# Sixteen routing weights per token: from selector products on TensorE to a DRAM row read back by DMA, with the preparing chain two steps earlier

## The chip, the cores and the metric

The kernel runs on one core of a Trainium2 chip as one program. The metric is the device time of one execution in microseconds; the times below are of separate executions of the same program.

## What is computed

The model has two layers on 2048 tokens of width 128: an attention layer with a mixture of eight experts, then a state-space mixer with a gated MLP, and at the end the mixture that this change touches. Cut to that last part (x is 2048 x 128, E = 16 experts, K = 8 of them chosen, plus one shared expert that every token uses):

```python
scores   = sigmoid(x @ gate_w.T)                 # 16 per token
inds     = top_k(scores + expert_bias, 8)
selected = scores[inds] / sum(scores[inds]) * 2.826
combine  = one_hot(inds) @ selected              # 16 weights per token, 8 of them zero
h        = silu(x @ w_gate[e].T) * (x @ w_up[e].T)
y        = sum_e combine[:, e] * (h[e] @ w_down[e].T)
y        = y + (silu(x @ shared_gate.T) * (x @ shared_up.T)) @ shared_down.T
out      = layernorm(x + y)
```

The kernel computes all sixteen experts for all tokens and multiplies the hidden activations of expert e by the token's weight for e before the down product.

## The kernel before

All of the change is in `mixer_tail_stage`, the last of the kernel's stages. It works on four blocks of 512 tokens (b = 0 to 3). The activations lie transposed, features on the 128 partitions and the 512 tokens of a block along the free dimension, so a token's routing weight has to be present on all partitions as a row of 512 numbers, one row per expert.

In each block there are 17 steps (x = 0 to 16, `NX`); step 0 is the shared expert and the others are experts 0 to 15. On TensorE a step has, in this order: the gate product (L1629, written G below), the up product (L1632, U), for x above 0 the selector product (L1639, S), and the down product of the step before (L1648, D). A number behind the letter is the step whose data it works on, so step 14 issues G14, U14, S14, D13. After step 16 an eighteenth turn of the loop (x = 17) has only D16. G, U and D are fp32 products of 128 x 128 weights with 512 columns, each two matmul instructions. S is one bf16 matmul: a 96 x 128 matrix of ones and zeros (`sel`) picks the row of one expert out of `cparts`, which holds the 16 x 512 weights in three bf16 parts on partitions 0, 32 and 64, and writes their sum on all 128 partitions of PSUM bank 4.

ScalarE applies silu to the gate product (L1755). VectorE multiplies it by the up product (L1906) and then by the spread weights in bank 4 (L1911, result `hid`); the two together are `hidden(b, x)`, and its end is called h of that step. S waits for h of the step before, since it overwrites bank 4, and so does D.

Between the steps of block b the chain that prepares block c = b + 1 is laid out by hand, with one piece per step on each engine in its own order. Its pieces before the change, with the step x behind which each stands on its engine:

- `turn_xs` (TensorE, 0), `copy_xs` (ScalarE, 1), `mean_squares` (VectorE, 0), `project` (TensorE, 2), `residual` (VectorE, 2), `square2` (ScalarE, 4), `mean_squares2` (VectorE, 4), a power on GpSimd (L1510), `scale` (VectorE, 6, L1835)
- `turn_n` (TensorE, 7), `copy_n` (ScalarE, 7), `gate_up`, `silu3` and `gated` (TensorE, ScalarE, VectorE, 8 to 10), `project_down` and `add_mlp` (11), `mean` (VectorE, 12), `apply` (ScalarE, 13), `turn_x` and `copy_x` (14)
- `route` (TensorE, 15, L1599), `sigmoid` (ScalarE, 15), `choose` (VectorE, 15, the top 8 of 16 and the normalised weights), `turn_c` (TensorE, 17, L1607), `parts` (VectorE, 16, L1884 to L1892)

From block 1 on, `turn_back` (TensorE, 4, L1619), `finish` (VectorE, 4, L1916), a power on GpSimd, `mean_out` (VectorE, 6) and `apply_out` (ScalarE, 7) finish block b - 1, and the sync engine stores it (L1499). `turn_xs` waits until `parts` of the block has read bank 7. All waits between engines are semaphores; an engine executes its own list in order, so a waiting instruction holds everything behind it.

Of the kernel before, what the change touches and what calls it, by code (L numbers as in the profile page):

```python
# [16 lines left out]
P = 128  # L17
# [1424 lines left out]
def mixer_tail_stage(g, m, out, eps=1e-5, eps_rms=1e-6):  # L1442
# [7 lines left out]
    with ExitStack() as ctx:  # L1450
# [18 lines left out]
        total = g.sb(ctx, "t3_total", [P, 4])  # L1469
        rest = g.sb(ctx, "t3_rest", [RE, 512])  # L1470
        cparts = g.sb(ctx, "t3_cparts", [96, 2, 512], BF16)
        sel = g.sb(ctx, "t3_sel", [96, RE * P], BF16)
        hid = g.sb(ctx, "t3_hid", [P, 2, 512])
# [10 lines left out]
        x_ps, x_sb, logits, sig = S_("x_turned"), S_("x_copied"), S_("logits"), S_("sigmoid")  # L1484
        routed, choice, c_turned, c_step, c_done = (S_(x) for x in ("route_step", "choice", "c_turned", "c_step", "c_parts"))
        zeroed, sel_in = S_("zeroed"), S_("sel_in")
        gu_ps, c_ps, acted, used, h_done, down = (S_(x) for x in ("gate_up", "c_spread", "silu", "used", "hid", "down"))
        out_sb, back, fin, var2, rstd2, nb2, sent = (S_(x) for x in ("out_copied", "back", "fin", "fvar", "frstd", "fmean", "final"))
# [3 lines left out]
        with nc.Block() as block:  # L1492
            @block.sync
            def _(sp):
                sp.dma_start(g.XW[:], g.aps["experts"]).then_inc(g.experts_in, 16)
                sp.dma_start(g.sel[:], g.aps["select"]).then_inc(g.experts_in, 16)
                for b in range(NB):
                    sp.wait_ge(sent, 4 * b + 4)
                    sp.dma_start(out.rearrange("o (t p) e -> p (o t) e", p=P)[:, 4 * b:4 * b + 4, :],  # L1499
                                 blk(g.X, b)).then_inc(stored, 16)  # L1500
                sp.wait_ge(stored, 16 * NB)

            @block.gpsimd
            def _(pool):
                half4 = g.half[:, 0:4]
                pool.memset(cparts[:], 0.0).then_inc(zeroed, 1)

                def power(dst, src, due, b, done):
                    pool.wait_ge(due, b + 1)
                    pool.tensor_tensor(dst, src, half4, ALU.pow).then_inc(done, 1)  # L1510
# [24 lines left out]
            def _(pe):  # L1535
                def turn_xs(b):

                    if b:
                        pe.wait_ge(sig, b)
                        pe.wait_ge(c_done, 5 * b - 1)  # L1540
                        if b >= 3:
                            pe.wait_ge(fin, b - 2)
# [79 lines left out]
                def products(b, x):  # L1622

                    e, k = order[x], NX * b + x
                    if k == 0:
                        pe.wait_ge(g.experts_in, 32)
                    if k >= 2:
# [4 lines left out]
                    pe.matmul(ps[:, 2 + k % 2, :], xw("up", e), XT[:, b % 2, :], start=True, stop=True).then_inc(gu_ps, 1)  # L1632
                    if x:
                        if x == 1:
                            pe.wait_ge(c_done, 5 * b + 5)
                        if k == 1:
                            pe.wait_ge(sel_in, 1)
# [22 lines left out]
                for b in range(NB):  # L1660
                    c = b + 1
                    for x in range(NX + 1):
# [22 lines left out]
                        if x == 17:  # L1685
                            turn_c(c)
# [3 lines left out]
            def _(act):  # L1690
# [86 lines left out]
                for b in range(NB):  # L1777
                    c = b + 1
                    for x in range(NX):
# [11 lines left out]
                        if x == 4:  # L1791
                            square2(c)
                        if x == 7:
                            copy_n(c)
                        if 8 <= x <= 10:
                            silu3(c, x - 8)
                        if x == 13:
                            apply(c)
                        if x == 14:
                            copy_x(c)  # L1800
                        if x == 15:
                            sigmoid(c)
# [4 lines left out]
            def _(dve):  # L1807
                stats = Count(stepped)
                routing = Count(routed)
                c_count = Count(c_step)  # L1810

# [63 lines left out]

                def parts(b):

                    part = lambda n: cparts[32 * n:32 * n + RE, b % 2, :]
                    dve.wait_ge(c_turned, b + 1)
                    if b == 0:  # L1880
                        dve.wait_ge(zeroed, 1)
                    if b >= 2:
                        dve.wait_ge(c_ps, RE * (b - 1))
                    dve.tensor_copy(part(0), B[0:RE, :]).then_inc(c_done, 1)  # L1884
                    dve.wait_ge(c_done, 5 * b + 1)
                    dve.tensor_tensor(rest[:], B[0:RE, :], part(0), ALU.subtract).then_inc(c_done, 1)
                    dve.wait_ge(c_done, 5 * b + 2)
                    dve.tensor_copy(part(1), rest[:]).then_inc(c_done, 1)
                    dve.wait_ge(c_done, 5 * b + 3)
                    dve.tensor_tensor(rest[:], rest[:], part(1), ALU.subtract).then_inc(c_done, 1)  # L1890
                    dve.wait_ge(c_done, 5 * b + 4)
                    dve.tensor_copy(part(2), rest[:]).then_inc(c_done, 1)  # L1892

                def hidden(b, x):
# [37 lines left out]
                choose(0)  # L1932
                parts(0)
                for b in range(NB):
                    c = b + 1
                    for x in range(NX):
# [11 lines left out]
                        if x == 4:  # L1948
                            mean_squares2(c)
                        if x == 6:  # L1950
                            scale(c)
                        if 8 <= x <= 10:
                            gated(c, x - 8)
                        if x == 11:
                            add_mlp(c)
                        if x == 12:
                            mean(c)
                        if x == 15:
                            choose(c)
                        if x == 16:  # L1960
                            parts(c)
                finish(NB - 1)
# [7 lines left out]
def layers(nc, aps, out):  # L1970
    with ExitStack() as ctx:
# [32 lines left out]
        with ExitStack() as mctx:  # L2004
# [10 lines left out]
            with ExitStack() as xctx:  # L2015
                g.XW = g.sb(xctx, "experts_w", [P, X_N])
                g.sel = g.sb(xctx, "select", [96, RE * P])
                g.experts_in = g.sem("experts_in")
                mixer_tail_stage(g, m, out)


def host_layout(inputs):
# [44 lines left out]
    for name in ("ident", "mask_qk", "mask_kq"):  # L2067
# [18 lines left out]
        "rope_cos": c32(cos), "rope_sin": c32(sin),  # L2086
        "select": np.repeat(np.tile(np.eye(32, RE), (3, 1)), P, axis=1).astype(np.float32),
    }
# [14 lines left out]
```

## Time and profile before

| what | value |
|---|---|
| median of 3 runs | 1882.82 us (1882.42 to 1883.24) |
| the profiled execution, its own time | 1885.1 us |
| its span, first to last instruction | 1883.3 us |
| TensorE busy | 1666.7 us, 88% |
| VectorE busy | 1335.5 us, 71% |
| ScalarE busy | 1141.9 us, 61% |
| GpSimd busy | 200.9 us, 11% |
| mean granted TensorE clock | 0.929 |

The last stage begins at about 1596 us of the span. Its four blocks of expert steps run from 1634 us to 1874 us. The span is 1.8 us shorter than the execution's own time, and that time is 2.3 us above the median of the runs. Matmul records overlap: a record lasts longer than the slot that the instruction takes in the queue, so slots are read from start to start.

### The profile page before, as it was taken

The numbers are of one execution on the slowest core, as the hardware profiler recorded it, in microseconds if no ns is written. First come the engines' busy times: TensorE is split into PE (matmuls) and PEld (weight loads), VectorE is DVE, ScalarE is ACT, GpSimd is POOL, SyncE is SP. The second block draws the span as 40 slices with busy tenths as digits, with TensorE's granted clock in tenths as the row PEclk, the third lists the DMA queues.
The fourth block names the chain that finished last, engine by engine and source line by source line (L and its number), as shares of the span: only waits on it lengthen the run. The fifth ranks groups of instructions, "written<-read, shape, count | busy, mean of one in ns | idle before, by whom it ended". The sixth has DMA issues, their size and how long they took to land. (4 is left out here: it accounts for less than half of the span.)

```text
span 1883.3 us, 25598 instructions
## 1 busy us (share of the span) xinstructions
PE 1666.7 (88%) x9916; PEld 795.1 (42%) x9916; DVE 1335.5 (71%) x1849; ACT 1141.9 (61%) x2305; POOL 200.9 (11%) x160
## 2 busy tenths in 40 slices
PE   6699999999999998857999999999794376699998
PEld 4233333333333333343444444455562344344443
DVE  4988888888888886258788677674474676355654
ACT  5078888888888887741677877777444511333432
POOL 1000000000000100110010001111522041100100
PEclk9699999999999999967899999999897777799999
DMA  2000000000000000010000000000000000100000
GB/s 94 0 1 1 1 1 1 1 1 1 1 1 1 1 1 1 1 45 0 1 1 1 1 1 1 2 1 2 1 1 0 0 1 27 61 1 6 6 1 12
DMA packets 4665, 13.32 MB, mean 7 GB/s; under 512 B 344, under 2 KB 2400, under 8 KB 4192
## 3 DMA queue, kind: packets, MB, share of 16 engines
q1 hardware_dynamic: 4544, 11.68, 1.9%
q8 instruction: 79, 1.29, 0.3%
q14 instruction: 42, 0.34, 0.1%
HBM read 10.63 MB, written 1.05 MB: 6 GB/s over the span
## 5 line engine op out<-in xcount | busy, mean ns | idle before, releaser
L636 DVE TENSOR_REDUCE a_part_max<-a_ps 128x2 f32<-128x1024 f32 x512 | 602.1, 1221 | 85.2 <-PE a_ps L495 84.4
L621 ACT ACTIVATE a_probs<-a_ps 128x512 f32<-128x512 f32 x1024 | 532.7, 615 | 128.7 <-PE a_ps L553 126.4
L636 DVE TENSOR_REDUCE f_part_max<-f_ps 128x2 f32<-128x1024 f32 (+3 forms) x320 | 327.3, 1061 | 121.6 <-PE f_ps L495 65.3
L553 PE MATMUL a_ps<-a_q_shift,a_KA 64*128 64x512 f32 x1024 | 366.0, 446 | 3.9 <-POOL a_q_shift L476 2.7
L621 ACT ACTIVATE f_probs<-f_ps 128x512 f32<-128x512 f32 (+3 forms) x640 | 300.3, 538 | 99.1 <-PE f_ps L553 48.6
L495 PE MATMUL a_ps<-a_KA,a_q_open 64*128 64x512 f32 x1024 | 285.0, 484 | 14.5 <-DVE a_part_max L636 13.8
L553 PEld LDWEIGHTS a_ps<-a_q_shift,a_KA 64*128 64x128 f32 x1024 | 166.9, 186 | 289.0 <-ACT a_probs L621 274.0
L571 PE MATMUL a_psO<-a_probs,a_VA 128*32 128x512 f32 x2048 | 274.6, 608 | 3.9 <-ACT a_probs L621 3.9
L553 PE MATMUL f_ps<-f_q_shift,f_KA 64*128 64x512 f32 (+3 forms) x640 | 222.9, 434 | 4.8 <-ACT f_probs L621 2.2
L495 PE MATMUL f_ps<-f_KA,f_q_open 64*128 64x512 f32 (+3 forms) x640 | 175.2, 452 | 17.0 <-DVE f_part_max L636 16.2
L553 PEld LDWEIGHTS f_ps<-f_q_shift,f_KA 64*128 64x128 f32 x640 | 106.6, 188 | 148.9 <-ACT f_probs L621 138.9
L495 PEld LDWEIGHTS a_ps<-a_KA,a_q_open 64*128 64x128 f32 x1024 | 124.7, 191 | 96.9 <-DVE a_part_max L636 77.3
L571 PE MATMUL f_psO<-f_probs,f_VA 128*32 128x512 f32 (+3 forms) x1280 | 152.2, 548 | 0.1
L1755 ACT ACTIVATE t_prod<-t_ps 128x512 f32<-128x512 f32 x68 | 40.6, 597 | 129.1 <-PE t_ps L1629 129.1
L476 POOL TENSOR_TENSOR a_q_shift<-a_q_open,a_shift_row 128x512 fp32r<-128x512 f32 x32 | 40.2, 1278 | 661.0 <-ACT a_shift_row L614 661.0
L495 PEld LDWEIGHTS f_ps<-f_KA,f_q_open 64*128 64x128 f32 x640 | 83.7, 196 | 44.9 <-DVE f_part_max L636 31.9
L1906 DVE TENSOR_TENSOR t_prod<-t_prod,t_ps 128x512 f32<-128x512 f32 x64 | 43.9, 687 | 68.7 <-PE t_ps L1632 68.7
L476 POOL TENSOR_TENSOR f_q_shift<-f_q_open,f_shift_row 128x512 fp32r<-128x512 f32 x32 | 40.1, 1275 | 424.3 <-ACT f_shift_row L614 424.3
L1648 PE MATMUL t_ps<-t_hid,experts_w 128*128 128x512 f32 x136 | 69.9, 594 | 5.2 <-DVE t_hid L1911 5.2
L1629 PE MATMUL t_ps<-t_XT,experts_w 128*128 128x512 f32 x136 | 70.6, 601 | 0.0
L1632 PE MATMUL t_ps<-t_XT,experts_w 128*128 128x512 f32 x136 | 70.3, 599 | 0.0
L571 PEld LDWEIGHTS a_psO<-a_probs,a_VA 128*32 128x32 f32 x2048 | 40.5, 108 | 70.6 <-issue 31.4
(311 smaller groups left out, 1765.2 us busy)
## 6 DMA issues: line engine op xcount, KB each, us to landing
experts_w<-in_experts SPq DMA_DIRECT2D x1, 3264.0 KB, 12.6
W<-in_weights SPq DMA_DIRECT2D x1, 2086.0 KB, 10.5
out<-X SPq DMA_DIRECT2D x4, 256.0 KB, 2.3
select<-in_select SPq DMA_DIRECT2D x1, 768.0 KB, 13.9
K<-in_consts SPq DMA_DIRECT2D x1, 644.0 KB, 7.0
R<-in_rows SPq DMA_DIRECT2D x1, 530.0 KB, 6.1
X<-in_x SPq DMA_DIRECT2D x1, 0.5 KB, 6.4
C<-in_cols SPq DMA_DIRECT2D x1, 15.0 KB, 5.3
```

The costliest lines, as they stand in the source:

```text
L476: pool.tensor_tensor(q_shift[:, u % 2, jp, :], q_open[:, u % 2, jp, :].bitcast(F32), shift_row[:, u % 2, :], ALU.add).then_inc(q_shifted, 1)
L495: mm = pe.matmul(ps1[:, k % 2, x, 0:b - a], q_open[rows, u % 2, jp, P * q:P * q + P], g.KA[rows, 2 * n + jp, a:b], start=True, stop=not diag)
L553: mm = pe.matmul(bank(r)[:, lo:512], g.KA[rows, 2 * n + jp, P * s:P * s + P], q_shift[rows, u % 2, jp, lo:512], start=True, stop=not diag)
L571: mm = pe.matmul(psO[32 * j:32 * j + 32, lo:hi], g.VA[:, s, VW * h:VW * h + 32], probs[:, st % 2, j, lo:hi], start=(s == 0), stop=(s == pl ...
L621: nc.scalar.activation(probs[:, st % 2, j, lo:512], bank(r)[:, lo:512], ACT.Exp, scale=SCALE).then_inc(ring_read, 1)
L636: dve.tensor_reduce(part_max[:, 4 * q + 2 * jp:4 * q + 2 * jp + 2, c], ps1[:, k % 2, :, 0:b - a], AX_X, ALU.max).then_inc(max_read, 1)
L1629: pe.matmul(ps[:, k % 2, :], xw("gate", e), XT[:, b % 2, :], start=True, stop=True).then_inc(gu_ps, 1)
L1632: pe.matmul(ps[:, 2 + k % 2, :], xw("up", e), XT[:, b % 2, :], start=True, stop=True).then_inc(gu_ps, 1)
L1648: pe.matmul(ps[:, 5, :], xw("down", order[x]), hid[:, k % 2, :], start=(x == 0), stop=(x == NX - 1)).then_inc(down, 1)
L1755: nc.scalar.activation(prod[:, k % 2, :], ps[:, k % 2, :], ACT.Silu).then_inc(acted, 1)
L1906: dve.tensor_tensor(p, p, ps[:, 2 + k % 2, :], ALU.mult).then_inc(used, 1)
```

## The change

The selector products, their matrix, and the splitting in three bf16 parts are removed. `copy_c` on VectorE copies the 16 x 512 weights of a block from PSUM to SBUF. The sync engine stores them to a DRAM tensor `c_rows` (32 KB), waits for the store, and reads them back onto all 128 partitions in four DMAs of four experts each (1 MB per DMA, 8 KB per partition) into `c_all`, which holds two blocks. `hidden` takes its second factor from `c_all`, and waits for one of the four DMAs at x = 1, 5, 9 and 13. From `turn_n` on the chain stands two steps earlier, `scale` one step earlier. The stores of results on the sync engine stand behind the weights' DMAs of two blocks on.

```diff
@@ sync engine
                 sp.dma_start(g.XW[:], g.aps["experts"]).then_inc(g.experts_in, 16)
-                sp.dma_start(g.sel[:], g.aps["select"]).then_inc(g.experts_in, 16)
                 for b in range(NB):
+                    sp.wait_ge(c_sb, b + 1)
+                    sp.dma_start(g.c_rows[b], cT[:, b % 2, :]).then_inc(c_out, 16)
+                    sp.wait_ge(c_out, 16 * b + 16)
+                    if b >= 2:
+                        sp.wait_ge(h_done, NX * (b - 1))
+                    for e in range(0, RE, 4):
+                        sp.dma_start(c_all[:, b % 2, e:e + 4, :],
+                                     g.c_rows[b, e:e + 4].partition_broadcast(P)).then_inc(c_in[e // 4], 16)
+                    if b < 2:
+                        continue
+                    sp.wait_ge(sent, 4 * b - 4)
+                    sp.dma_start(out..[:, 4 * b - 8:4 * b - 4, :], blk(g.X, b - 2)).then_inc(stored, 16)
+                for b in range(NB - 2, NB):
                     sp.wait_ge(sent, 4 * b + 4)
                     sp.dma_start(out..[:, 4 * b:4 * b + 4, :], blk(g.X, b)).then_inc(stored, 16)
@@ GpSimd
-                pool.memset(cparts[:], 0.0).then_inc(zeroed, 1)
-                    if b == 0:
-                        pool.wait_ge(g.experts_in, 32)
-                        pool.tensor_copy(sel[:], g.sel[:]).then_inc(sel_in, 1)
@@ TensorE: turn_xs and products
-                        pe.wait_ge(c_done, 5 * b - 1)
+                        pe.wait_ge(c_sb, b)
-                    if x:
-                        if x == 1:
-                            pe.wait_ge(c_done, 5 * b + 5)
-                        pe.wait_ge(h_done, k)
-                        pe.matmul(ps[:, 4, :], sel[:, P * e:P * e + P], cparts[:, b % 2, :],
-                                  start=True, stop=True).then_inc(c_ps, 1)
@@ TensorE: order
-                        if x == 7:
+                        if x == 5:
                             turn_n(c)
-                        if 8 <= x <= 10:
-                            gate_up(c, x - 8)
-                        if x == 11:
+                        if 6 <= x <= 8:
+                            gate_up(c, x - 6)
+                        if x == 9:
                             project_down(c)
-                        if x == 14:
+                        if x == 12:
                             turn_x(c)
+                        if x == 13:
+                            route(c)
                         if x == 15:
-                            route(c)
-                        if x == 17:
                             turn_c(c)
@@ ScalarE: order (copy_n 7 to 5, silu3 8..10 to 6..8, apply 13 to 11, copy_x 14 to 12, sigmoid 15 to 13)
@@ VectorE
-                def parts(b):                       # five operations, L1884 to L1892
+                def copy_c(b):
                     dve.wait_ge(c_turned, b + 1)
                     if b >= 2:
+                        dve.wait_ge(c_out, 16 * (b - 1))
+                    dve.tensor_copy(cT[:, b % 2, :], B[0:RE, :]).then_inc(c_sb, 1)
@@ hidden
-                    dve.wait_ge(c_ps, n)
+                    if (x - 1) % 4 == 0:
+                        dve.wait_ge(c_in[(x - 1) // 4], 16 * b + 16)
-                    dve.tensor_tensor(h, p, ps[:, 4, :], ALU.mult).then_inc(h_done, 1)
+                    dve.tensor_tensor(h, p, c_all[:, b % 2, order[x], :], ALU.mult).then_inc(h_done, 1)
@@ VectorE: order (scale 6 to 5, gated 8..10 to 6..8, add_mlp 11 to 9, mean 12 to 10, choose 15 to 13,
   parts at 16 to copy_c at 14)
```

## Rows read from the trace of the kernel before

**Rows 1.** Windows: length, busy us of PE, PEld, DVE, ACT, POOL, granted clock, DMA.

```profile
1640.00:1690.00 50.00, 50.00 (x161) 24.75 (x159) 25.20 (x48) 15.62 (x35) 3.30 (x3) 1.00 0.00 0
1690.00:1702.00 12.00, 9.38 (x38) 4.92 (x37) 8.84 (x30) 5.95 (x14) 0.05 (x1) 1.00 0.01 2
```

**Rows 2.** Timeline of PE, one step of block 3: start, us, what.

```profile
1865.70 0.38 PE L1639 MATMUL t_ps<-t_cparts,t_sel 96*128 96x512 bf16 x1
1865.92 1.02 PE L1648 MATMUL t_ps<-t_hid,experts_w 128*128 128x512 f32 x2
1866.78 1.02 PE L1629 MATMUL t_ps<-t_XT,experts_w 128*128 128x512 f32 x2
```

**Rows 3.** Group by line: count, busy us, mean ns, idle before.

```profile
L1911 DVE TENSOR_TENSOR t_hid<-t_prod,t_ps 128x512 f32<-128x512 f32 x64 | 43.9, 687 | 2.2
```

**Rows 4.** Timeline of PE, end of block 0 to start of block 1.

```profile
1691.02 0.96 PE L1599 MATMUL t_ps<-W,t_XT 128*128 128x16 f32 x8
...
1693.84 1.02 PE L1648 MATMUL t_ps<-t_hid,experts_w 128*128 128x512 f32 x2
1696.46 1.13 PE L1648 MATMUL t_ps<-t_hid,experts_w 128*128 128x512 f32 x2 [1.59 <-DVE t_hid L1911]
1697.42 0.60 PE L1607 MATMUL t_ps<-K,t_score 128*16 128x128 f32 x4
1697.86 1.02 PE L1629 MATMUL t_ps<-t_XT,experts_w 128*128 128x512 f32 x2
...
1700.77 1.06 PE L1545 MATMUL t_ps<-K,m_xs 128*128 128x128 f32 x8 [1.02 <-DVE t_rest L1890]
```

**Rows 5.** Timeline of PE, the waits around block 3.

```profile
1828.93 0.38 PE L1639 MATMUL t_ps<-t_cparts,t_sel 96*128 96x512 bf16 x1 [0.47 <-DVE t_hid L1903]
...
1872.95 1.13 PE L1648 MATMUL t_ps<-t_hid,experts_w 128*128 128x512 f32 x2 [0.42 <-DVE t_hid L1911]
```

**Rows 6.** Timeline of DVE, the stretch of Rows 4.

```profile
1695.72 0.69 DVE L1911 TENSOR_TENSOR t_hid<-t_prod,t_ps 128x512 f32<-128x512 f32 x1
1698.06 0.68 DVE L1884 CAST t_cparts<-t_ps 16x512 bf16<-16x512 f32 x1 [1.66 <-PE t_ps L1607]
```

**Rows 7.** Timeline of DVE in block 0, `hidden` of step 6 and `scale`.

```profile
1656.27 0.69 DVE L1906 TENSOR_TENSOR t_prod<-t_prod,t_ps 128x512 f32<-128x512 f32 x1 [1.39 <-PE t_ps L1632]
...
1657.60 0.68 DVE L1835 TENSOR_TENSOR t_normed<-Y,t_rms 128x512 f32<-128x512 f32 x1
```

**Rows 8.** Timeline of PE, DVE and POOL, step 5 of block 1.

```profile
1715.07 1.02 PE L1629 MATMUL t_ps<-t_XT,experts_w 128*128 128x512 f32 x2
...
1718.18 0.69 DVE L1911 TENSOR_TENSOR t_hid<-t_prod,t_ps 128x512 f32<-128x512 f32 x1
...
1717.63 1.01 POOL L1510 TENSOR_TENSOR t_rms<-t_ss,minus_half 128x4 f32<-128x4 f32 x1 [14.68 <-DVE t_ss L1827]
1718.61 1.01 POOL L1510 TENSOR_TENSOR t_rstd<-t_var,minus_half 128x4 f32<-128x4 f32 x1
```

**Rows 9.** Timelines of POOL and DVE, both reading SBUF, stage before.

```profile
1527.88 1.11 POOL L1293 TENSOR_TENSOR ss_al<-K,ss_a 128x512 f32<-128x512 f32 x1 [1.98 <-PE ss_ps L1312]
...
1528.33 1.21 DVE L1414 TENSOR_TENSOR ss_seg<-ss_seg,ss_gm 128x512 f32<-128x512 f32 x1
```

**Rows 10.** DMA issues: KB each, median us from issue to landing.

```profile
experts_w<-in_experts SPq DMA_DIRECT2D x1, 3264.0 KB, 12.6
...
out<-X SPq DMA_DIRECT2D x4, 256.0 KB, 2.3
...
R<-in_rows SPq DMA_DIRECT2D x1, 530.0 KB, 6.1
```

**Rows 11.** Windows, load stage; the last two numbers are DMA share and GB/s.

```profile
8.00:10.00 2.00, 0.00 (x0) 0.00 (x0) 0.00 (x0) 0.00 (x0) 0.00 (x0) 1.00 1.11 436
```

**Rows 12.** Timelines of DVE and PE, start of block 0.

```profile
1634.31 0.68 DVE L1884 CAST t_cparts<-t_ps 16x512 bf16<-16x512 f32 x1 [1.11 <-PE t_ps L1607]
...
1638.59 1.02 PE L1629 MATMUL t_ps<-t_XT,experts_w 128*128 128x512 f32 x2
```

More of the change, by code:

```diff
@@ L1469, in mixer_tail_stage @@
         total = g.sb(ctx, "t3_total", [P, 4])
-        rest = g.sb(ctx, "t3_rest", [RE, 512])
-        cparts = g.sb(ctx, "t3_cparts", [96, 2, 512], BF16)
-        sel = g.sb(ctx, "t3_sel", [96, RE * P], BF16)
+        cT = g.sb(ctx, "t3_cT", [RE, 2, 512])
+        c_all = g.sb(ctx, "t3_c_all", [P, 2, RE, 512])
         hid = g.sb(ctx, "t3_hid", [P, 2, 512])
@@ L1484, in mixer_tail_stage @@
         x_ps, x_sb, logits, sig = S_("x_turned"), S_("x_copied"), S_("logits"), S_("sigmoid")
-        routed, choice, c_turned, c_step, c_done = (S_(x) for x in ("route_step", "choice", "c_turned", "c_step", "c_parts"))
-        zeroed, sel_in = S_("zeroed"), S_("sel_in")
-        gu_ps, c_ps, acted, used, h_done, down = (S_(x) for x in ("gate_up", "c_spread", "silu", "used", "hid", "down"))
+        routed, choice, c_turned, c_sb = (S_(x) for x in ("route_step", "choice", "c_turned", "c_copied"))
+        c_out, c_in = S_("c_stored"), [S_("c_spread%d" % n) for n in range(4)]
+        gu_ps, acted, used, h_done, down = (S_(x) for x in ("gate_up", "silu", "used", "hid", "down"))
         out_sb, back, fin, var2, rstd2, nb2, sent = (S_(x) for x in ("out_copied", "back", "fin", "fvar", "frstd", "fmean", "final"))
@@ L1495, in _ @@
                 sp.dma_start(g.XW[:], g.aps["experts"]).then_inc(g.experts_in, 16)
-                sp.dma_start(g.sel[:], g.aps["select"]).then_inc(g.experts_in, 16)
                 for b in range(NB):
+                    sp.wait_ge(c_sb, b + 1)
[9 more added lines that the diff above has]
+                    sp.wait_ge(sent, 4 * b - 4)
+                    sp.dma_start(out.rearrange("o (t p) e -> p (o t) e", p=P)[:, 4 * b - 8:4 * b - 4, :],
+                                 blk(g.X, b - 2)).then_inc(stored, 16)
+                for b in range(NB - 2, NB):
                     sp.wait_ge(sent, 4 * b + 4)
@@ L1625, in products @@
                     if k == 0:
-                        pe.wait_ge(g.experts_in, 32)
+                        pe.wait_ge(g.experts_in, 16)
                     if k >= 2:
@@ L1632, in products @@
                     pe.matmul(ps[:, 2 + k % 2, :], xw("up", e), XT[:, b % 2, :], start=True, stop=True).then_inc(gu_ps, 1)
-                    if x:
-                        if x == 1:
-                            pe.wait_ge(c_done, 5 * b + 5)
-                        if k == 1:
-                            pe.wait_ge(sel_in, 1)
-                        pe.wait_ge(h_done, k)
-                        pe.matmul(ps[:, 4, :], sel[:, P * e:P * e + P], cparts[:, b % 2, :],
-                                  start=True, stop=True).then_inc(c_ps, 1)
                 def sum_down(b, x):
@@ L1792, in _ @@
                             square2(c)
-                        if x == 7:
+                        if x == 5:
                             copy_n(c)
-                        if 8 <= x <= 10:
-                            silu3(c, x - 8)
+                        if 6 <= x <= 8:
+                            silu3(c, x - 6)
+                        if x == 11:
+                            apply(c)
+                        if x == 12:
+                            copy_x(c)
                         if x == 13:
[L1798 to L1801, printed above, removed]
                             sigmoid(c)
@@ L1809, in _ @@
                 routing = Count(routed)
-                c_count = Count(c_step)
                 def mean_squares(b):
@@ L1874, in choose @@
                     dve.tensor_tensor(score[:], score[:], over_cols(total[:], RE), ALU.mult).then_inc(choice, 1)
-                def parts(b):
-                    part = lambda n: cparts[32 * n:32 * n + RE, b % 2, :]
+                def copy_c(b):
                     dve.wait_ge(c_turned, b + 1)
-                    if b == 0:
-                        dve.wait_ge(zeroed, 1)
                     if b >= 2:
[L1883 to L1892, printed above, removed]
+                        dve.wait_ge(c_out, 16 * (b - 1))
+                    dve.tensor_copy(cT[:, b % 2, :], B[0:RE, :]).then_inc(c_sb, 1)
                 def hidden(b, x):
@@ L1932, in _ @@
                 choose(0)
-                parts(0)
+                copy_c(0)
                 for b in range(NB):
@@ L1949, in _ @@
                             mean_squares2(c)
-                        if x == 6:
+                        if x == 5:
                             scale(c)
-                        if 8 <= x <= 10:
-                            gated(c, x - 8)
-                        if x == 11:
+                        if 6 <= x <= 8:
+                            gated(c, x - 6)
+                        if x == 9:
                             add_mlp(c)
-                        if x == 12:
+                        if x == 10:
                             mean(c)
-                        if x == 15:
+                        if x == 13:
                             choose(c)
-                        if x == 16:
-                            parts(c)
+                        if x == 14:
+                            copy_c(c)
                 finish(NB - 1)
@@ L2016, in layers @@
                 g.XW = g.sb(xctx, "experts_w", [P, X_N])
-                g.sel = g.sb(xctx, "select", [96, RE * P])
+                g.c_rows = nc.dram_tensor("c_rows", (NB, RE, 512), F32, kind="Internal").ap()
                 g.experts_in = g.sem("experts_in")
@@ L2086, in host_layout @@
         "rope_cos": c32(cos), "rope_sin": c32(sin),
-        "select": np.repeat(np.tile(np.eye(32, RE), (3, 1)), P, axis=1).astype(np.float32),
     }
```

## The prediction

> **What bounds the kernel now.** I read the windows first. In the expert steps TensorE is busy 50.00 of 50 us at the full granted clock (1.00, the 2.4 GHz level), while VectorE has work for half of the time; between two blocks TensorE is busy 9.38 of 12 us and the clock stays at 1.00 [rows 1]. So a step costs what TensorE's slots add up to, and besides it only waits at the turn of blocks count. I then read slots in the timeline, from start to start. S takes 1865.92 - 1865.70 = 0.22 us, D takes 0.86 [rows 2], and G and U are the same kind of product as D. A step is 3 x 0.86 + 0.22 = 2.80 us, against 2 x 0.69 us on VectorE [rows 3].
>
> At the turn of blocks 0 and 1 D15 ends at 1693.84 + 0.86 = 1694.70 and D16 starts at 1696.46, a gap of 1.76 us, because `choose` stands ahead of `hidden(16)`; D16's own slot is then 0.96, 0.10 more than unstalled. G and U of the next block end at 1697.86 + 1.72 = 1699.58 and `turn_xs` starts at 1700.77, a gap of 1.19 us, for `parts` [rows 4]. Together 3.05 us. The turn of blocks 1 and 2 repeats this. At the third there is no `turn_xs`; the second wait is listed with 0.47 instead of 1.02 us [rows 4, 5], so I count 2.50. The waits sum to 8.6 us.
>
> **Removed: the selectors.** 64 x 0.22 = 14.1 us, if nothing takes their place in the step. What could is VectorE's answer: it starts 0.20 us after a TensorE slot ends (turn_c ends at 1697.86, the cast starts at 1698.06), and a waiting D starts 0.05 us after h (1695.72 + 0.69 against 1696.46) [rows 4, 6]. From the end of U to its D that is 0.20 + 0.72 + 0.69 + 0.05 = 1.66 us. The next G and U and the D before them cover 2.58 us, so 0.9 us is spare. At the very end of the kernel D16 has only D15 (0.86) as cover: its gap grows from 0.58 (0.42 listed, and the 0.16 by which a record outlasts its slot [rows 2, 5]) to 0.80. Loss 0.2 us. The second product reads SBUF instead of PSUM; `scale`, with two SBUF operands of the same size, takes 0.68 against 0.69 us [rows 3, 7], so nothing is gained there. The GpSimd memset and cast and the matrix's load lie ahead of the blocks beside other work: nothing.
>
> **Moved: choose and turn_c.** I lay the turn out from the start of `route`, with the old pieces. `route`, G14 and U14 take 1693.84 - 1691.02 - 0.22 = 2.60 us [rows 4], D13 ends at 3.46, G15 and U15 at 5.18. `choose` is as long as before: D behind it can start 1696.46 - 1691.02 = 5.44 us after `route`. Gap 0.26 where it was 1.76, since two products now stand in it. D14 ends at 6.35, `turn_c` (0.44) at 6.79, `copy_c` runs from 6.99 to 7.67 (0.68, as the cast [rows 6]). It is ahead of `hidden(15)`, whose h ends at 7.70 + 1.41 = 9.11, while G16 and U16 end at 8.51: gap 0.65. D15 ends at 10.12, h16 at 10.55: gap 0.48; D16 ends at 11.56. `turn_xs` then waits for nothing. Gaps 1.39 and three restarts of about 0.08 make 1.63 us per turn, 4.9 in three, against 8.6. Gain 3.7 us.
>
> **Moved: scale and turn_n, now both at x = 5.** This is what is late next. Before, `scale` stood at 6 and `turn_n` at 7, with a whole step as cover. In block 0 `scale` starts 1657.60 - 1656.27 = 1.33 us after `hidden` starts and takes 0.68 [rows 7]. So it ends 0.20 + 1.33 + 0.68 = 2.21 us after U5, and TensorE, which has only D4 (0.86) in between, waits 1.40 us. In blocks 1 and 2 `finish` is ahead of `hidden(5)`: G5 starts at 1715.07 and h5 ends at 1718.87, 3.80 us later [rows 8]; `scale` ends 0.60 us after that and `turn_n` can start at 4.45, while G5, U5 and D4 are over at 2.58. Wait 1.87 us, twice. With three restarts of 0.1 the loss is 1.40 + 3.74 + 0.30 = 5.4 us. All later pieces keep their distances from each other; `mean_out` and `apply_out`, which stay at 6 and 7, now fall beside `gated` and `silu3`. `apply_out` is some 1.6 us on ScalarE behind silu(7), whose next customer is a gate product three slots (2.58 us) behind G7: covered.
>
> **A new neighbour on VectorE.** In the stage before, a VectorE product with two SBUF operands started at 1528.33 beside a GpSimd operation that lasted until 1528.99, and took 1.21 us, ending 0.55 us after GpSimd's end [rows 9]; alone such a product takes 0.69. The second product of `hidden` becomes one of these. In block 1 it starts at 1718.18 beside GpSimd's powers (1717.63 to 1718.64, 1718.61 to 1719.62) [rows 8], and `scale` follows it, with TensorE waiting. If only the first power holds it up, it ends some 0.3 us later; if the second power goes ahead of `scale` as well, `scale` ends 1.25 us later. Twice: between 0.6 and 2.5 us. Below it is 0, if a power on 4 columns holds nothing. I take 1.5, between the waits that the one 512-column row would give. Other powers meet products with 0.5 us or more to spare.
> The Trainium skill (SBUF — State Buffer, section "SBUF: two separate sides") says the same: a VectorE operation with two SBUF inputs and a GpSimd operation that reads SBUF exclude each other for the whole instruction. By that rule in full the sum would lose 2.5 us here instead of 1.5.
>
> **Added: store and read back.** The nearest store, 256 KB, lands in 2.3 us [rows 10]; at 436 GB/s, the rate in the load stage while the rows were being broadcast to all partitions [rows 11], 0.6 us of it is data, so 1.7 is fixed and 32 KB take 1.8. A load of 1.05 MB takes 1.7 + 2.4 = 4.1 us by the same two numbers. The upper bound is from the experts' load: 12.6 us [rows 10], of which 3.34 MB at 436 GB/s are 7.7, leaves 4.9 fixed: 7.3 us.
> In block 0 `copy_c` takes the place of the first cast and ends at 1634.99; G1 starts at 1638.59 [rows 12], so D1 can start five slots later, at 1642.89, and needs the first load 0.74 us before, at 1642.15. Store, wait and issue bring it to 1636.9 + L. It may take 5.3 us: no wait with L = 4.1, 2.0 us with 7.3. In blocks 1 to 3 `copy_c` ends at 7.67 and the load starts to be issued at 9.57; D1 could start at 11.56 + 1.72 + 0.9 (turn_xs) + 4.3 = 18.48, and needs it by 17.7, so L may be 8.2: no wait at either end. Loads 2 to 4 come 2.4 us apart and are wanted four steps (over 10 us) apart. Sync's stores of results queue behind the loads, but are not awaited before the end. I take 0, ends 0 and 2.0.
> The Trainium skill (DMA: Bandwidth & Descriptors, section "Bandwidth") gives 6.15 us for a 1 MB load from GpSimd's queue; an estimate by that figure has 0.9 us of wait in block 0.
>
> **Sum.** -14.1 (selectors) + 0.2 (end) - 3.7 (turns) + 5.4 (`turn_n`) + 1.5 (GpSimd) + 0 (loads) = -10.7 us. Made on the profiled execution (1885.1, span 1883.3), it gives 1874.4 there; the median of the runs is 2.3 lower, so 1882.8 - 10.7 = 1872.1. Two tenths of a per cent, 3.8 us, is about what a measurement can tell from no change.
>
> **Rivals.**
> - Both new costs at their upper ends (2.5 and 2.0 us): -7.7, 1875.1. For it: the full hold-up in [rows 9] and the slow experts' load. Chance 0.15.
> - `turn_n` does not wait (TensorE has work I overlooked, or the records place `scale` too late): -16.1, 1866.7. Against it: the order in the queue leaves only D4. Chance 0.07.
> - The other side: the first load is late. The broadcast reads the same 8 KB 128 times; if it runs slowly, every block waits at h1. The waits sum to (L - 5.3) + 3(L - 8.2), which eats 10.7 us at L = 10.2, a rate of about 125 GB/s. At 75 GB/s L is 15.7 and the waits are 32.9 us: 1905. Against it: 436 GB/s beside the rows' broadcast [rows 11]. Chance 0.08.
> - The change doesn't shorten the step: another wait, D on h, fills the selector's slot. 1872.1 + 14.1 = 1886. Against it: 0.9 us to spare. Chance 0.03.
>
> The forecast has the remaining 0.67, with its terms between 1869 and 1876. To leave no more than 2 in 10 out I reach from 1866 to 1879. Faster by over 0.2%: the forecast, the first two rivals and the lesser late loads less a little for mis-sized terms, 0.86; within 0.2% 0.05; slower 0.09.
>
> **What the profile after would show.** Steps of 2.58 us from G to G. TensorE idle ahead of `turn_n` (L1561 before), released by `scale`, 1.4 us in block 0 and 2 to 3 in blocks 1 and 2. Gaps of 0.3, 0.7 and 0.5 us at D14, D15, D16, none at `turn_xs`. VectorE's second product near 0.69 us alone and over 1 us beside GpSimd. First load landing 4 to 7 us after issue. The prediction is wrong if VectorE stands idle at x = 1 waiting for a DMA, or if a moved piece waits that I called covered.

## The result and the profile after

The changed kernel takes 1870.93 us (median of 4 runs, 1870.26 to 1871.63); the kernel before, in the same session, 1883.03 us (1882.42 to 1883.90). The ratio is 0.9935, with a 95% interval of 0.9918 to 0.9953: 12.1 us faster, beyond the 0.2% that a measurement can tell. The forecast was 1872.1 us with a range of 1866 to 1879.

The two profiled executions differ by more than that, 1885.1 against 1870.26 us, because the last stage begins at 1596.53 us in the one and at 1594.34 us in the other, with the same instructions ahead of it. The stage's own instructions start alike: `turn_c` of block 0 starts 36.72 us behind the issue of the experts' load in both. So all comparisons of profiles below use the length of the last stage alone, from the issue of the experts' load (the stage's first DMA) to the end of the span. It is 1883.3 - 1596.53 = 286.8 us before and 1868.5 - 1594.34 = 274.2 us after: 12.6 us less. The waits are read as in the prediction: from the end of one slot (0.86 us behind a product's start, 0.96 behind a restart) to the next start.

The timeline of TensorE, kernel after, at the end of the kernel (start, us of the record, what):

```profile
1853.85 1.02 PE L1647 MATMUL t_ps<-t_hid,experts_w 128*128 128x512 f32 x2
...
1856.43 1.02 PE L1647 MATMUL t_ps<-t_hid,experts_w 128*128 128x512 f32 x2
1858.10 1.12 PE L1647 MATMUL t_ps<-t_hid,experts_w 128*128 128x512 f32 x2 [0.65 <-DVE t_hid L1899]
```

From one D to the next it is 2.58 us, where [rows 2] add up to 2.80. D16 starts 1858.10 - 1856.43 - 0.86 = 0.81 us late (0.58 before [rows 5], 0.80 forecast).

The turn of blocks 0 and 1, same view; `route` is L1606, `turn_c` L1614, `turn_xs` L1552:

```profile
1681.82 0.96 PE L1606 MATMUL t_ps<-W,t_XT 128*128 128x16 f32 x8
...
1686.15 1.02 PE L1639 MATMUL t_ps<-t_XT,experts_w 128*128 128x512 f32 x2
1687.27 1.12 PE L1647 MATMUL t_ps<-t_hid,experts_w 128*128 128x512 f32 x2
1688.24 0.60 PE L1614 MATMUL t_ps<-K,t_score 128*16 128x128 f32 x4
...
1689.53 1.02 PE L1639 MATMUL t_ps<-t_XT,experts_w 128*128 128x512 f32 x2
1690.93 1.12 PE L1647 MATMUL t_ps<-t_hid,experts_w 128*128 128x512 f32 x2 [0.37 <-DVE t_hid L1899]
1692.25 1.13 PE L1647 MATMUL t_ps<-t_hid,experts_w 128*128 128x512 f32 x2 [0.20 <-DVE t_hid L1899]
...
1694.93 1.04 PE L1552 MATMUL t_ps<-K,m_xs 128*128 128x128 f32 x8
```

The gaps are 0.26, 0.54 and 0.36 us at D14, D15 and D16, and none at `turn_xs`. Against [rows 4], the one long wait at D16 has become three short ones, and the wait at `turn_xs` is gone; the other two turns show the same three numbers within 0.01.

And `turn_n` (L1568), in block 0 and in block 1:

```profile
1650.19 1.02 PE L1647 MATMUL t_ps<-t_hid,experts_w 128*128 128x512 f32 x2
1652.46 0.66 PE L1568 MATMUL t_ps<-K,t_normed 128*128 128x128 f32 x4 [1.25 <-DVE t_normed L1833]
...
1710.05 1.02 PE L1647 MATMUL t_ps<-t_hid,experts_w 128*128 128x512 f32 x2
1712.82 0.66 PE L1568 MATMUL t_ps<-K,t_normed 128*128 128x128 f32 x4 [1.74 <-DVE t_normed L1833]
```

These are the new waits: 1652.46 - 1651.05 = 1.41 us, and 1712.82 - 1710.91 = 1.91 us, and 1.90 in block 2. The prediction had 1.4 us in block 0 and named 2 to 3 in the others.

VectorE and GpSimd at step 5 of block 1, the stretch that answers to [rows 8]; first GpSimd's two powers, then VectorE's second product of `hidden(5)` and `scale`:

```profile
1710.92 1.01 POOL L1520 TENSOR_TENSOR t_rms<-t_ss,minus_half 128x4 f32<-128x4 f32 x1 [12.69 <-DVE t_ss L1825]
1711.90 1.12 POOL L1520 TENSOR_TENSOR t_rstd<-t_var,minus_half 128x4 f32<-128x4 f32 x1
```

```profile
1711.47 0.69 DVE L1899 TENSOR_TENSOR t_hid<-t_prod,t_c_all 128x512 f32<-128x512 f32 x1
1712.08 0.68 DVE L1833 TENSOR_TENSOR t_normed<-Y,t_rms 128x512 f32<-128x512 f32 x1
```

The second product has two SBUF operands now, starts inside a power, and takes 0.69 us. `scale` starts beside the other power and takes 0.68. VectorE was held up by nothing here; the second power took 0.11 us longer than the first.

The DMA issues (KB each, median us from issue to landing), and the first use of a loaded weight on VectorE, in block 0:

```profile
t_c_all<-c_rows SPq DMA_DIRECT2D x16, 1024.0 KB, 8.0
...
c_rows<-t_cT SPq DMA_DIRECT2D x4, 32.0 KB, 1.6
```

```profile
1639.16 0.69 DVE L1899 TENSOR_TENSOR t_hid<-t_prod,t_c_all 128x512 f32<-128x512 f32 x1 [0.17 <-DMA t_c_all<-c_rows]
```

Of the sixteen loads the quickest landed 4.6 us after its issue and the slowest 11.5; the four of a block are issued within 3 us of each other. VectorE waited for a load once, 0.17 us at step 1 of block 0, and D1 of block 0 was not late: h1 came at 1639.85 and D1 was due at 1640.67, behind U2. The prediction had named an idle VectorE at x = 1 as a sign that it is wrong. To the letter the sign came, but the wait lies inside TensorE's cover and costs nothing.

### The profile page after: what moved, and what is told of

Its sections match the earlier page's. It is cut to its first block and busy times, and to the rows that moved or that the text cites. A ratio compares the mean times of both kernels' runs of the same rounds, so it can differ in the third digit from the quotient of the medians.

```text
span 1868.5 us, 25468 instructions
## 1 busy us (share of the span) xinstructions
PE 1653.2 (88%) x9852; PEld 786.8 (42%) x9852; DVE 1325.5 (71%) x1833; ACT 1141.9 (61%) x2305; POOL 198.6 (11%) x158
## 6 DMA issues: line engine op xcount, KB each, us to landing
experts_w<-in_experts SPq DMA_DIRECT2D x1, 3264.0 KB, 11.8
```

## The experiments

The stage lengths are from one profiled execution each. The medians are of 4 runs, except for the two kernels that were run once. They come from several sessions, each with its own runs of the kernel before (1883.03 to 1884.07 us), so kernels are best compared by the ratio or by the stage.

| kernel | median us | ratio to before (95%) | last stage us |
|---|---|---|---|
| before | 1883.03 | | 286.8 |
| after | 1870.93 | 0.9935 (0.9918 to 0.9953) | 274.2 |
| e8_selector_twice | 1896.62 | 1.0069 (1.0054 to 1.0084) | 299.7 |
| e1_unmoved | 1872.72 | 0.9943 (0.9928 to 0.9957) | 274.8 |
| e2_move_only | 1893.88 | 1.0050 (1.0034 to 1.0067) | 296.3 |
| e4_one_step | 1872.24 | 0.9940 (0.9926 to 0.9955) | 275.9 |
| e3_one_load | 1898.88 (once) | | 303.5 |
| e6_no_reload | 1871.00 | 0.9934 (0.9918 to 0.9951) | 274.1 |
| e5_pool_512 | 1873.86 (once) | | 277.6 |
| v1_turn_n_between | 1866.83 | 0.9909 (0.9894 to 0.9923) | 269.9 |
| v2a_carry | 1864.70 | 0.9902 (0.9886 to 0.9919) | 268.4 |
| v2_between_carry_act | 1863.22 | 0.9890 (0.9875 to 0.9905) | 266.5 |

**The selectors, doubled.** On the kernel before:

```diff
+                        pe.matmul(ps[:, 4, :], sel[:, P * e:P * e + P], cparts[:, b % 2, :], start=True, stop=True)
                         pe.matmul(ps[:, 4, :], sel[:, P * e:P * e + P], cparts[:, b % 2, :],
                                   start=True, stop=True).then_inc(c_ps, 1)
```

> The kernel before with every selector product issued twice into the same bank. If a selector costs its slot of 0.22 us and nothing covers it, 64 more cost 14.0 us: 1896 to 1898 us. If part of it lay beside a wait, less: under 1892 us.

The stage grew by 299.7 - 286.8 = 12.9 us, the median by 13 us against the 1883.67 of its session. That is 60 slots of 0.215 us, not 64: at each of the four last steps the gap ahead of D16 shrank by one slot, from 1.76 to 1.54 us at the turns and from 0.58 to 0.37 us at the end. S16 lay in the cover of a wait. The other sixty are paid in full. Steps show the same: between steps without a wait the distance from D to D is 2.796 us before (30.75 us over 11 steps of block 3), 3.010 here and 2.576 in the changed kernel. So the second of two selectors costs 0.215 us, and taking the only one away saves 0.220.

**The change without the move.** On the changed kernel, the chain at its old steps:

```diff
-                        if x == 5:
+                        if x == 7:
                             turn_n(c)
...
-                        if x == 13:
+                        if x == 15:
                             choose(c)
-                        if x == 14:
+                        if x == 16:
                             copy_c(c)
```

> The change with the chain left at its old steps (turn_n 7, choose 15, copy_c 16, turn_c 17): weights by DMA, no selectors. My theory (moving the chain gains at the turns about what turn_n's new wait costs): no TensorE wait ahead of turn_n; at each turn a gap of 1.98 us at D16, and the first load of blocks 1 to 3, which now starts to be issued about 1.8 us after turn_c, lands about 0.9 us too late for D1 with turn_xs in between and 1.8 us without it. About 9.5 us of such waits against 9.9 in the changed kernel: 1870 to 1872 us. Rival (the move is what makes the DMA usable): the store and load stand open by 4 to 8 us in each block, 1883 to 1895 us.

TensorE and VectorE at the first load of block 1 (same columns as above):

```profile
1698.41 1.02 PE L1639 MATMUL t_ps<-t_XT,experts_w 128*128 128x512 f32 x2
1700.86 1.13 PE L1647 MATMUL t_ps<-t_hid,experts_w 128*128 128x512 f32 x2 [1.43 <-DVE t_hid L1899]
```

```profile
1700.11 0.69 DVE L1899 TENSOR_TENSOR t_hid<-t_prod,t_c_all 128x512 f32<-128x512 f32 x1 [2.53 <-DMA t_c_all<-c_rows]
```

D1 waited 1.59, 0.92 and 1.47 us for the load in blocks 1 to 3, D16 waited 1.98 us at each turn, and `turn_n` did not wait. The stage is 0.6 us longer than with the move, and the intervals of the two ratios overlap. So the load is exposed without the move, but by 4.0 us in all and not by 4 to 8 us per block, and what the move saves at the turns and at the loads it pays back at `turn_n`. All but 0.6 us of the gain can be had without the second half of the change.

**The move without the change.** On the kernel before, the chain at its new steps, selectors and `parts` kept:

```diff
-                        if x == 16:
+                        if x == 14:
                             parts(c)
```

> The kernel before with only the chain moved (selectors and the bf16 parts kept). My theory: turn_n waits 1.2 us in block 0 and 1.65 in blocks 1 and 2, 4.8 us with restarts; the turns lose about 1 us, since the five operations of parts (3.0 us) now stand ahead of hidden(15): 1887 to 1890 us. Rival (the earlier chain is itself a gain and the selectors' removal gave less than 14 us): 1880 to 1882 us.

The direction was right, the size not: the stage grew by 9.5 us instead of 5 to 7. `turn_n` waited 1.19, 1.66 and 1.66 us, as expected. Ahead of S16 stood one gap of 2.98 us per turn, since S16 waits for h15 behind `parts` (TensorE's timeline, first turn and middle turn):

```profile
1697.78 0.39 PE L1639 MATMUL t_ps<-t_cparts,t_sel 96*128 96x512 bf16 x1 [2.82 <-DVE t_hid L1911]
1698.01 3.16 PE L1648 MATMUL t_ps<-t_hid,experts_w 128*128 128x512 f32 x4
...
1765.08 2.22 PE L1648 MATMUL t_ps<-t_hid,experts_w 128*128 128x512 f32 x4
1767.13 1.02 PE L1629 MATMUL t_ps<-t_XT,experts_w 128*128 128x512 f32 x2
```

The four matmuls of D15 and D16 take 2.95 us to the next start (1700.96) at the first turn and 2.05 (1767.13) at the middle one. The granted clock fell after this gap and after that of the last turn (0.72 in 1700 to 1704, 0.58 in 1832 to 1836), not after the middle one. From S16 of one turn to S16 of the next it is 67.07 us where the clock fell and 65.53 where it didn't: 1.5 us. Two falls are 3.1 of the 3.7 us that the expectation (4.8 + 1) lacked.

Together with the run of the change without the move, the four combinations of the two halves are complete. The move alone costs 9.5 us where the selectors and `parts` are kept and gains 0.6 where they are gone; the removal is worth 12.0 us without the move (286.8 - 274.8) and 22.1 with it (296.3 - 274.2). The gains of the two halves don't add up.

**One step instead of two.** On the changed kernel:

```diff
-                        if x == 5:
+                        if x == 6:
                             turn_n(c)
...
-                        if x == 13:
+                        if x == 14:
                             choose(c)
-                        if x == 14:
+                        if x == 15:
                             copy_c(c)
```

> The changed kernel with the chain moved one step instead of two (scale stays at 5, turn_n 6, choose 14, copy_c 15, turn_c 16). My theory: turn_n has G6, U6 and D5 as cover and does not wait (-5.4 us); the turns have one product step less ahead of hidden(16), gaps 0.26 and 2.3 us instead of 0.26, 0.54 and 0.36, so +1.3 us each; the first load still lands 2 us before it is needed: 1868.5 to 1870 us. Rival (turn_n's wait is only a shifted wait and comes back elsewhere): 1871 us or more.

It came out at 1872.24 us and the stage at 275.9, 1.7 us longer than with two steps instead of 1.5 shorter (-5.4 + 3 x 1.3, of the expectation). The waits are the expected ones: none at `turn_n`, 0.26 at D15 and 2.25 us at D16. But the clock fell after two of the three gaps of 2.25 us. TensorE's timeline at the second turn, and the windows around it (busy us of PE, PEld, DVE, ACT, POOL, granted clock, DMA):

```profile
1749.78 0.60 PE L1614 MATMUL t_ps<-K,t_score 128*16 128x128 f32 x4
1752.47 2.01 PE L1647 MATMUL t_ps<-t_hid,experts_w 128*128 128x512 f32 x2 [2.09 <-DVE t_hid L1899]
1754.27 1.88 PE L1636 MATMUL t_ps<-t_XT,experts_w 128*128 128x512 f32 x2
1755.98 1.03 PE L1639 MATMUL t_ps<-t_XT,experts_w 128*128 128x512 f32 x2
```

```profile
1748.00:1752.00 4.00, 2.28 (x8) 0.66 (x6) 2.28 (x5) 0.49 (x1) 0.00 (x0) 1.00 0.01 2
1752.00:1756.00 4.00, 3.53 (x5) 1.47 (x6) 0.42 (x1) 0.00 (x0) 0.00 (x0) 0.57 0.48 195
```

D16 and G0 take 1.80 and 1.71 us instead of 0.96 and 0.86, so a fall costs about 1.7 us here, and two of them make the 3.2 us by which the expectation missed. So the expected waits came, and of the two theories' times the rival's (1871 us or more), though not by its mechanism: no wait came back elsewhere. I had priced waits by their length alone.

**One load of 4 MB.** On the changed kernel:

```diff
-                    for e in range(0, RE, 4):
-                        sp.dma_start(c_all[:, b % 2, e:e + 4, :],
-                                     g.c_rows[b, e:e + 4].partition_broadcast(P)).then_inc(c_in[e // 4], 16)
+                    sp.dma_start(c_all[:, b % 2], g.c_rows[b].partition_broadcast(P)).then_inc(c_in[0], 16)
...
-                    if (x - 1) % 4 == 0:
+                    if x == 1:
```

> The changed kernel with one 4 MB load per block instead of four of 1 MB, awaited at x = 1. My theory (D1 can take the load up to 5.5 us after its issue in block 0 and 8.2 us in the others; the rate is 430 GB/s): the load lands 12 us after issue, TensorE waits 6.5 us at D1 in block 0 and 3.8 us in blocks 1 to 3, 18 us in all: 1887 to 1891 us. Rival (the engines run ahead and make most of it up, or the broadcast is slow and lands far later): under 1880 or over 1900 us.

The loads landed 11.8 to 13.2 us after issue (median 12.3). D1 waited 6.41, 5.05, 4.28 and 4.95 us, 20.7 in all, against 18 expected. The stage is 29.3 us longer than that of the changed kernel; the other 8.6 us are the clock, which fell after each of the four. From D1 to `turn_n` (in block 3 to D16) it takes 2.8, 1.7, 2.6 and 1.6 us longer than in the changed kernel, and the size doesn't follow the length of the gap. Block 0, TensorE's timeline and the windows (busy us by engine, granted clock, DMA):

```profile
1646.32 2.08 PE L1645 MATMUL t_ps<-t_hid,experts_w 128*128 128x512 f32 x2 [6.25 <-DVE t_hid L1897]
```

```profile
1644.00:1648.00 4.00, 1.69 (x2) 0.84 (x3) 1.98 (x3) 0.00 (x0) 0.00 (x0) 0.65 0.00 0
1648.00:1652.00 4.00, 4.00 (x18) 3.75 (x17) 0.16 (x1) 0.00 (x0) 0.00 (x0) 0.50 0.00 0
```

The late load was the mechanism of the rival on the other side, and this run shows it: without the cut in four the kernel is slower than the one before (1898.88 us in its one run, against 1883.11 to 1885.18 in seven).

**No loads in blocks 1 to 3.** On the changed kernel:

```diff
-                    for e in range(0, RE, 4):
+                    for e in range(0, RE if b == 0 else 0, 4):
...
-                    if (x - 1) % 4 == 0:
+                    if (x - 1) % 4 == 0 and b == 0:
...
-                    dve.tensor_tensor(h, p, c_all[:, b % 2, order[x], :], ALU.mult).then_inc(h_done, 1)
+                    dve.tensor_tensor(h, p, c_all[:, 0, order[x], :], ALU.mult).then_inc(h_done, 1)
```

> The changed kernel with the loads of the weights left out in blocks 1 to 3 (they use the weights of block 0; this leaves 12.6 MB of DMA out, the stores stay). My theory (12.6 MB of SBUF writes cost the engines nothing, and no wait on them ended last): the same as the changed kernel, 1870 to 1872 us, all durations unchanged. Rival (the traffic slows the engines or a load is waited for): 1 to 4 us faster.

Median 1871.00 against 1870.93, stage 274.1 against 274.2, and the gaps the same within 0.01 us. 12.6 MB of DMA beside the products cost nothing that these runs can tell.

**A wide addition on GpSimd.** On the changed kernel, behind the power for rms2:

```diff
+                    pool.tensor_tensor(spare[:, 0, :], spare[:, 1, :], spare[:, 1, :], ALU.add)
```

> The changed kernel with a GpSimd addition of 128 x 512 elements of SBUF (1.27 us, on a buffer that nothing uses) behind the power for rms2 in blocks 0 to 2, and a memset of that buffer at the stage's start. It tests why the powers held nothing up. If two SBUF operands on VectorE and a GpSimd operation exclude each other only while GpSimd streams its data, the addition holds up the second product of hidden(5) or scale by 0.5 to 1.2 us in blocks 1 and 2, and turn_n's wait grows from 1.91 to 2.4 to 3.1 us, where the power of 4 columns added nothing. If there is no exclusion in this stage, all second products stay at 0.69 us and turn_n's wait at 1.91.

GpSimd and VectorE in block 1; `scale` is L1837 here:

```profile
1712.10 1.16 POOL L1536 TENSOR_TENSOR t_spare<-t_spare 128x512 f32<-128x512 f32 x1
```

```profile
1711.66 0.69 DVE L1903 TENSOR_TENSOR t_hid<-t_prod,t_c_all 128x512 f32<-128x512 f32 x1
1712.27 1.53 DVE L1837 TENSOR_TENSOR t_normed<-Y,t_rms 128x512 f32<-128x512 f32 x1
```

`scale` took 1.53 us instead of 0.68 and ended 0.54 us after the addition did, as the product in [rows 9] did. In block 0 the second product took 0.84 us and ended 0.55 behind the addition. `turn_n` waited 1.56, 2.75 and 2.74 us instead of 1.41, 1.91 and 1.90. So VectorE is held up by a GpSimd operation that streams 512 columns, and not by a power on 4 columns that lasts as long. Here too the clock fell, after one of the two gaps (0.79 in 1712 to 1720, 1.00 in 1772 to 1780): the stage is 3.4 us longer, where the waits grew by 1.8.

**turn_n between U6 and D5.** On the changed kernel:

```diff
                         if x < NX:
                             products(b, x)
+                        if x == 6 and c < NB:
+                            turn_n(c)
                         if x:
                             sum_down(b, x - 1)
...
-                        if x == 5:
-                            turn_n(c)
...
-                        if x == 5:
+                        if x == 6:
                             copy_n(c)
```

> The changed kernel with turn_n (TensorE) issued between U6 and D5 and copy_n (ScalarE) behind silu(6), all else at its new step. My theory: D4, G6 and U6 (2.58 us) cover scale, turn_n does not wait, D5 covers copy_n: -5.4 us, 1865 to 1866.5 us. Rival (D5 or gate_up waits for copy_n or h instead): 1868 us or more.

The stage is 4.3 us shorter, not 5.4. In blocks 1 and 2 a gap of 0.19 us is left: `scale` is ready 4.45 us after G5 starts, and G5, U5, D4, G6 and U6 end at 4.30. I had called it covered without adding that up. And the first of the gate and up products behind D5 (L1580) waits for `copy_n` in all three blocks (block 1, TensorE):

```profile
1714.43 1.02 PE L1647 MATMUL t_ps<-t_hid,experts_w 128*128 128x512 f32 x2
1715.37 1.12 PE L1580 MATMUL t_ps<-t_NT,W 128*128 128x512 f32 x2
1716.34 1.02 PE L1583 MATMUL t_ps<-t_NT,W 128*128 128x512 f32 x2
```

That is 1715.37 - 1715.29 = 0.08 us and a restart of 0.10 each time, 0.5 in three; with 0.48 for the two gaps at `turn_n` and their restarts it makes the 1.1 us that are missing, within 0.1. The median, 1866.83 us, lies between the two theories' numbers. The profile gives most of it to the first, and a small part to the rival's wait for `copy_n`.

This run also shows the hold-up of [rows 9] between two operations of the kernel itself, GpSimd's addition behind `scale` (L1536, Y<-Y,X, 128 x 512) and the second product of `hidden(6)`. In block 1 the addition starts at 1714.12 and takes 1.26 us; the product starts at 1714.67 and takes 1.27 us instead of 0.69, so it ended 0.56 us behind the addition. In the changed kernel the same addition runs from 1713.00 to 1714.27, where VectorE has nothing to do until 1715.23: the wait at `turn_n` keeps the two apart. The prediction, which looked at the powers alone, did not name this addition.

**The next block's first products ahead of D16.** On top of the last version:

```diff
-                        if x < NX:
+                        if x < NX and not (b and x == 0):
                             products(b, x)
+                        if x == NX and c < NB:
+                            products(c, 0)
```

> turn_n between U6 and D5 as in the kernel before this one, and besides the gate and up products of the next block's shared expert are issued ahead of D16, so that two products stand between D15 and D16. My theory: D16's gap (0.36 us) and its restart (0.10) go in three turns, D15's gap (0.54) stays: 1.4 us under the version with turn_n alone, by the last stage of the profile 268.4 us instead of 269.9. Rival (XT, bank or semaphore order makes the early products wait): no change or slower.

1864.70 us, stage 268.4 as expected. D16's gap is gone, D15's is 0.54 still.

**And copy_c on ScalarE.** On top of that, taken out of VectorE's order and put into ScalarE's behind silu(15):

```diff
-                        if x == 14:
-                            copy_c(c)
...
+                        if x == 15:
+                            copy_c(c)
```

> The same, and copy_c done by ScalarE behind silu(15) instead of VectorE ahead of hidden(15). My theory: D15's gap of 0.54 us and its restart go as well, since h15 no longer stands behind turn_c; only D14's gap of 0.26 is left at a turn: 3.3 us under the version with turn_n alone, last stage 266.5 us, median 1862.5 to 1864.5. Rival (the copy on ScalarE delays silu(16) and the load comes too late for D1): 1866 us or more.

1863.22 us (1862.29 to 1863.60), stage 266.5 as expected. The turn of blocks 0 and 1, TensorE:

```profile
1685.65 1.12 PE L1647 MATMUL t_ps<-t_hid,experts_w 128*128 128x512 f32 x2
1686.61 0.60 PE L1614 MATMUL t_ps<-K,t_score 128*16 128x128 f32 x4
1687.05 1.02 PE L1636 MATMUL t_ps<-t_XT,experts_w 128*128 128x512 f32 x2
1687.91 1.02 PE L1639 MATMUL t_ps<-t_XT,experts_w 128*128 128x512 f32 x2
1688.77 1.02 PE L1647 MATMUL t_ps<-t_hid,experts_w 128*128 128x512 f32 x2
1689.63 1.02 PE L1636 MATMUL t_ps<-t_XT,experts_w 128*128 128x512 f32 x2
1690.49 1.02 PE L1639 MATMUL t_ps<-t_XT,experts_w 128*128 128x512 f32 x2
1691.35 1.02 PE L1647 MATMUL t_ps<-t_hid,experts_w 128*128 128x512 f32 x2
1692.20 1.04 PE L1552 MATMUL t_ps<-K,m_xs 128*128 128x128 f32 x8
```

Behind `turn_c` the slots follow one another at 0.86 us up to `turn_xs`. This version beats both kernels, the one before by 1.1% and the changed one by 7.7 us of the stage.

## Why the prediction was right, step by step

- **The bound.** TensorE's slots bound the steps before and after; a step shortened by just the selector's slot (2.796 to 2.576 us), and doubling the selectors lengthened it by 0.215. Confirmed.
- **Selectors, -14.1 us.** The steps of 11 in a row shortened by 0.220 each, so 64 are 14.1. Four of the 64 lay ahead of waits; the layout of the turns and of the end had that in it, since it counted gaps anew.
- **End, +0.2 us.** 0.81 - 0.58 = 0.23.
- **Turns, -3.7 us.** Three gaps of 0.26, 0.54 and 0.36 were laid out as 0.26, 0.65 and 0.48. With 0.31 us of restarts a turn costs 1.47 us; before, the three cost 8.55. Gain 4.1 us, 0.4 more than forecast. The two small errors have one cause: on VectorE consecutive operations overlap by 0.07 us (`copy_c` starts at 1688.87 and takes 0.68, the next product starts at 1689.48), and I had put them end to end.
- **turn_n, +5.4 us.** 1.41 + 1.91 + 1.90 and three restarts of 0.05 make 5.4. Confirmed, and its cause too: placed behind G6 and U6 it vanishes in block 0 and is 0.19 us in the others.
- **GpSimd, +1.5 us.** This is the term that failed: 0. It took the hold-up of one row with 512 columns [rows 9] for a power on 4. The lower end that the step had named, a power that holds nothing, was the case. The wide additions, the one that was put in and the kernel's own, show that the hold-up itself is real. The same step had `turn_n` waiting 2 to 3 us in blocks 1 and 2, and it waited 1.91.
- **Loads, 0.** The first landed in 4.6 us where 4.1 was worked out and 5.3 allowed. The store took 1.6 us, not 1.8. The rate of 436 GB/s was that of a window in which the constants, the rows and the weights were all on their way, so it did not show what a broadcast alone does; the loads of this stage do (389 to 446 GB/s). Neither the late load nor the traffic cost anything.

By the terms as measured the sum is -14.1 + 0.2 - 4.1 + 5.4 = -12.6, which is what the profiles show; the medians say 12.1. The forecast of -10.7 was 1.9 us short by the profiles, 1.5 of it the GpSimd term and 0.4 the turns, and 1.4 by the medians.

Two things the prediction did not say. It priced the move as -3.7 + 5.4, a net loss, without drawing the conclusion that the chain could have stayed; the run with the chain unmoved is within 0.6 us of the changed kernel. And the price of the late-load rival left the clock out: 20.7 us of waits cost 29.3.

## What to carry to other kernels

When a chain is woven by hand into a loop that one engine bounds, moving it as a block moves its tight links too. Check for each piece what the bounding engine has left to do between the producer's last input and the consumer, and add up that cover in slots; here the move put `scale` and `turn_n` at the same step, which left only D4 (0.86 us) between them, and all but 0.19 us of the wait went when `turn_n` was put behind the next two products.

A broadcast through DRAM can take a copying job off a bound engine for nothing, if the first piece to be used is small enough to land inside the slack and the rest queues behind it: four loads of 1 MB cost nothing here where one of 4 MB made the stage 29 us longer.

Price a wait of the matmul engine in the profile with the granted clock beside it. Here a single gap of 1.98 us cost its length and a restart of 0.1, and one of 2.25 us cost 1.7 us more in two of three cases.

## What the runs showed of the hardware

- **Gaps and the clock.** In the expert steps at full clock (1.00, the 2.4 GHz level), none of the gaps of up to 1.98 us was followed by a fall of the granted clock, in any kernel. Of the twelve gaps from 2.25 to 6.41 us (three of 2.25, two of 2.75, three of 2.98, four of 4.28 to 6.41) nine were followed by one; the first products after a fall took twice their slot, the 1.2 GHz level. A fall cost 1.5 to 1.7 us beyond the gap after the shorter ones and 1.6 to 2.8 after those of 4 us and more. Why the same gap made the clock fall in one block and not in the next is open.
- **VectorE beside GpSimd.** A VectorE product with two SBUF operands, 0.69 us alone, ended 0.54 to 0.56 us after a GpSimd addition of 512 columns of SBUF beside it; beside a power on 4 columns, which lasts about as long, it took 0.69 (all 64 second products of the changed kernel, those beside powers among them, lie between 0.691 and 0.693 us). The Trainium skill (SBUF — State Buffer, section "SBUF: two separate sides") has GpSimd hold the shared ports for the whole instruction; the wide addition agrees, the narrow power doesn't.
- **Broadcast loads.** 1 MB from an 8 KB piece of DRAM onto 128 partitions landed 4.6 us after issue at the quickest, and 4 MB in 11.8 to 13.2 us. Between 1636 and 1644 us of the changed kernel, while block 0's loads ran, the DMA moved 389 to 446 GB/s, against 436 in [rows 11]. A 32 KB store landed in 1.6 us.
